# Local attention in a software pipeline: outputs moved one step later and behind the scores

## What is computed

```python
for i in range(DEPTH):                                            # 6 layers, 16 heads of 64
    x = attn_layer(shift_tokens(x), Wqkv[i], q_scale[i], k_scale[i], Wo[i]) + x
    x = ffn_layer(shift_tokens(x), ln_g[i], ln_b[i], W1[i], b1[i], W2[i], b2[i]) + x
# attn_layer: q, k, v = x @ Wqkv; q, k normalised by head, scaled, rotated
# each window of 32 queries sees its own 32 keys and the 32 before (masked to a band of 33)
sim = jnp.einsum('bhwie,bhwje->bhwij', bq, bk2) * QK_SCALE
attn = jax.nn.softmax(jnp.where(mask, -big, sim), -1)
out = jnp.einsum('bhwij,bhwje->bhwie', attn, bv2)                 # then out @ Wo
```

## Time and profile before

| what | value |
|---|---|
| median of three executions | 2394.74 us |
| the profiled execution | 2394.71 us |
| its span, first to last instruction | 2392.9 us |
| PE, matmuls | 2003.8 us (84%) |
| DVE | 1759.8 us (74%) |
| ACT | 1492.5 us (62%) |
| POOL | 1241.6 us (52%) |
| copies of line 822, first to last | 168.5 to 1916.4 us, 384 of them |

### The profile page before, as it was taken

How to read it: one execution, slowest core, us unless ns; L and a number is a source line. 1 busy time by engine, 2 the same in 40 slices (tenths; PEclk the granted TensorE clock), 3 DMA queues, 4 the chain that set the end, 5 groups by cost and what they waited for, 6 DMA issues and landing times. The chain is left out here.

```text
span 2392.9 us, 81109 instructions
## 1 busy us (share of the span) xinstructions
PE 2003.8 (84%) x33532; PEld 1489.2 (62%) x33532; DVE 1759.8 (74%) x3964; ACT 1492.5 (62%) x5173; POOL 1241.6 (52%) x869
## 2 busy tenths in 40 slices
PE   5549998999999999999998999989999964773377
PEld 2338767677676877758767577775877732432255
DVE  4568878688786887868778688786887837685754
ACT  2228768587685877858778587785877823451122
POOL 1138757477574776738767377673765701221000
PEclk8679999999999999999999999999999986885699
DMA  2011111021110211102111021110210100001000
GB/s 96 0 36 39 33 37 50 27 67 35 37 54 24 71 30 42 50 24 70 30 42 50 24 66 33 44 47 24 66 30 26 39 3 12 1 0 54 1 0 18
DMA packets 88157, 85.58 MB, mean 36 GB/s; under 512 B 15360, under 2 KB 82944, under 8 KB 87168
## 3 DMA queue, kind: packets, MB, share of 16 engines
q1 hardware_dynamic: 87808, 80.62, 11.9%
HBM read 25.51 MB, written 1.05 MB: 11 GB/s over the span
## 5 line engine op out<-in xcount | busy, mean ns | idle before, releaser
L1000 POOL TENSOR_TENSOR RN<-N,minus_half 128x8 f32<-128x8 f32 x384 | 632.7, 1648 | 179.8 <-DVE N L928 179.8
L840 ACT ACTIVATE PB<-PS,NMX 128x64 f32<-128x64 f32 x1536 | 462.0, 313 | 26.8 <-DVE NMX L948 10.0
L596 PE MATMUL PS<-WQ,XS 128*128 128x256 f32 x1536 | 434.5, 406 | 14.5 <-SPq L541 13.0
L995 POOL TENSOR_TENSOR RR<-R 128x512 f32<-128x512 f32 x192 | 244.6, 1274 | 151.6 <-DVE QK L958 151.6
L995 POOL TENSOR_TENSOR RR<-R1B,R2B 128x512 f32<-128x512 f32 x192 | 244.5, 1274 | 140.4 <-DVE QK L958 140.4
L840 ACT ACTIVATION_READ_ACCUMULATOR PB<-PS,NMX 128x1 f32 x1536 | 312.0, 203 | 0.0
L596 PEld LDWEIGHTS PS<-WQ,XS 128*128 128x128 f32 x1536 | 261.3, 190 | 69.8 <-SPq L541 13.3
L735 PE MATMUL PS<-XB,VS 64*64 64x32 f32 x6144 | 213.6, 223 | 91.4 <-ACT XB L817 91.4
L948 DVE TENSOR_REDUCE NMX<-PS 128x4 f32<-128x256 f32 x384 | 163.1, 425 | 172.2 <-PE PS L749 172.2
L735 PEld LDWEIGHTS PS<-XB,VS 64*64 64x64 f32 x6144 | 181.0, 134 | 147.1 <-issue 142.7
L958 DVE SCALAR_TENSOR_TENSOR QK<-RN,RR 128x512 f32<-128x512 f32 x384 | 261.9, 682 | 0.6 <-POOL RR L995 0.6
(11 more groups left out here) (212 smaller groups left out, 3715.0 us busy)
## 6 DMA issues: line engine op xcount, KB each, us to landing
VS<-XB SPq DMA_DIRECT2D x384, 96.0 KB, 2.1
VS<-XB SPq DMA_DIRECT2D x288, 32.0 KB, 2.6
WQ<-in_wqkv SPq DMA_DIRECT2D x40, 192.0 KB, 2.4
WO<-in_wo SPq DMA_DIRECT2D x6, 512.0 KB, 4.5
XS<-XT SPq DMA_DIRECT2D x10, 256.0 KB, 3.2
XS<-XT SPq DMA_DIRECT2D x10, 255.8 KB, 4.8
BIG<-in_wgu SPq DMA_DIRECT2D x1, 2048.0 KB, 8.3
W<-in_w SPq DMA_DIRECT2D x6, 341.0 KB, 4.2
```

The costliest lines, as they stand in the source:

```text
L596: mm = nc.tensor.matmul(PQ[:, m % 2, j * 256:(j + 1) * 256], XSb[b][:, t0:t0 + P], WQ[:, pair * 384:pair * 384 + 256], start=True, stop=True)
L840: ex = nc.scalar.activation(PB[:, g % 2, u, :], SC[:, h, DH * t:DH * t + DH], ACT.Exp, bias=NMX[:, u:u + 1], accum_out=PSUMS[:, g % 2, u:u ...
L995: nc.gpsimd.tensor_tensor(RR[:, :, :], R1k[(g + 1) % 2][:, :, :], R2k[(g + 1) % 2][:, :, :], ALU.add)\
L1000: nc.gpsimd.tensor_tensor(RN[:, g % 2, :], N2[:, g % 2, :], minus_half[:, :], ALU.pow)
```

## The change

In a step, the matmuls of the outputs now belong to chunk g-3 (before: g-2) and come behind the scores (before: ahead of them); the values that are projected in step g are those of chunk g (before: g+1). The transposes of q and k always come first, then those of the probabilities and the values. ACT copies in the order TQ (822), PO (828, now chunk g-4), PX (817); before it was PX, TQ, PO. SP waits on `vp_in`, the copy itself, in place of `v_in`, which is gone. PE's wait for the copy of PX moves to just ahead of the next use of PX, in the next step. The feed-forward part moves from g % 32 == 1 to 2, its second down projection to another bank, and the loops run one step longer. No operation is added to or taken from a chunk.

```diff
-                return (k // B, k % B) if k >= 0 and g % SLOT == 1 else None
+                return (k // B, k % B) if k >= 0 and g % SLOT == 2 else None
-            WOUT, TOKS, FEAT, DOWN = (2, 5), (3, 5), (4, 2), (5, 0)
+            WOUT, TOKS, FEAT, DOWN = (2, 5), (3, 5), (4, 2), (5, 1)
@@ SyncE
                         if there(g + 1):
-                            sp.wait_ge(v_in.sem, v_in.take())
+                            sp.wait_ge(vp_in.sem, g + 2)
@@ TensorE: project_qk, feed_forward
-                        if m > SLOT and m % SLOT == 6:
+                        if m > SLOT and m % SLOT == 7:
                         project(0, range(PAIRS))
+                        if probs:
+                            pe.wait_ge(vp_in.sem, vp_in.peek(1))
                         project(1, range(3))
@@ TensorE: step
-                        values, probs, ffn, tail = (there(g + 1), there(g - 2), feed_forward_at(g),
+                        values, probs, ffn, tail = (there(g), there(g - 2), feed_forward_at(g),
...
-                        if tail:
-                            qk_to_features()
-                            values_and_probabilities()
-                        else:
-                            values_and_probabilities()
-                            qk_to_features()
+                        if there(g):
+                            pe.wait_ge(qk_in.sem, qk_in.take())
...
+                            tr.then_inc(qkt_ps.sem, 1)
                         if tail:
+                            pe.wait_ge(gelu_free.sem, gelu_free.peek(2))
+                        if there(g - 1) or there(g - 3):
+                            pe.wait_ge(vp_in.sem, vp_in.take())
+                        if there(g - 3):
+                            pe.wait_ge(vs_in.sem, vs_in.take())
+                        if probs:
+                            pe.wait_ge(pn_in.sem, pn_in.take())
...
-                        if values or probs:
-                            pe.wait_ge(vp_in.sem, vp_in.take())
-                        if values:
-                            pe.sem_inc(v_in.sem, 1)
-                        if probs:
-                            c = (g - 2) % CH
-                            if g - 2 > 0:
-                                pe.wait_ge(o_free.sem, o_free.take())
...
-                            mm.then_inc(o_ps.sem, 1)
                         if there(g):
                             c = g % CH
                             pe.wait_ge(qkt_in.sem, qkt_in.take())
...
                             mm.then_inc(sc_in.sem, 1)
+                        if there(g - 3):
+                            c = (g - 3) % CH
+                            if g - 3 > 0:
+                                pe.wait_ge(o_free.sem, o_free.take())
...
+                            mm.then_inc(o_ps.sem, 1)
@@ ScalarE
+                    def outputs(m):
+                        l, b, pair, c = where(m)
+                        act.wait_ge(o_ps.sem, o_ps.take())
...
                     def step(g):
-                        values, probs = there(g + 1), there(g - 2)
-                        if values or probs:
...
-                            nc.scalar.activation(XB[:, (g + 1) % CH, cols], PX[:, cols], ACT.Copy)\
-                                .then_inc(vp_in.sem, 1)
+                        values, probs = there(g), there(g - 2)
                         if there(g):
...
                                 TQ.rearrange("p (k s) -> p k s", k=2), ACT.Copy).then_inc(qkt_in.sem, 1)
-                        if there(g - 2):
...
+                        if there(g - 4) and not feed_forward_at(g - 1):
+                            outputs(g - 4)
+                        if values or probs:
...
+                            nc.scalar.activation(XB[:, g % CH, cols], PX[:, cols], ACT.Copy)\
+                                .then_inc(vp_in.sem, 1)
...
                         if feed_forward_at(g):
+                            outputs(g - 3)
                             feed_forward(*feed_forward_at(g), g)
@@ all engines
-                    for g in range(-3, TOTAL + 3):
+                    for g in range(-3, TOTAL + 4):
```

More of the change, by code:

```diff
@@ L578, in _ @@
                                 load_layer(done[0] + 1)
-                    for f in (wq_dma, v_in, vs_dma, qks_free, layer_dma, qks_dma):
+                    for f in (wq_dma, vs_dma, qks_free, layer_dma, qks_dma):
                         f.settle(sp)
@@ L610, in feed_forward @@
                     def feed_forward(l, b, g):
+                        probs = there(g - 2)
                         def project(h, heads):
@@ L673, in step @@
                             project_qk(g + 3)
[L674 to L681, removed]
@@ new lines, in step @@
+                        if tail:
+                            pe.wait_ge(gelu_free.sem, gelu_free.peek(2))
[5 more added lines that the diff above has]
+                            pe.wait_ge(pn_in.sem, pn_in.take())
+                            for h in range(2):
+                                last = nc.tensor.transpose(
+                                    PX[:, 256 + h * P:256 + (h + 1) * P],
+                                    PB[:, g % 2, 2 * h:2 * h + 2, :].rearrange("p t k -> p (t k)"),
+                                    ident[:, :])
@@ new lines, in step @@
+                        if values:
+                            l, b, pair, c = where(g)
+                            for j in range(CB):
+                                t0 = (CB * c + j) * P
+                                last = nc.tensor.matmul(PX[:, j * P:(j + 1) * P], XSb[b][:, t0:t0 + P],
+                                                        WQ[:, pair * 384 + 256:(pair + 1) * 384],
+                                                        start=True, stop=True)
+                        if values or probs:
+                            last.then_inc(vp_ps.sem, 1)
@@ L754, in step @@
                             mm.then_inc(sc_in.sem, 1)
+                        if there(g - 3):
+                            c = (g - 3) % CH
+                            if g - 3 > 0:
+                                pe.wait_ge(o_free.sem, o_free.take())
+                            for w in range(4):
+                                for t in range(2):
+                                    for h in range(2):
+                                        keys = slice(2 * WIN * t, 2 * WIN * t + 2 * WIN)
+                                        vals = VX if w % 2 else VS
+                                        cols = 256 + P * h + WIN * w
+                                        mm = nc.tensor.matmul(
+                                            PO[DH * h:DH * h + DH, t, WIN * w:WIN * w + WIN],
+                                            vals[keys, c, w // 2, DH * h:DH * h + DH],
+                                            XB[keys, (g - 1) % CH, cols:cols + WIN],
+                                            start=True, stop=True)
+                            mm.then_inc(o_ps.sem, 1)
                         if ffn:
@@ L824, in step @@
                                 TQ.rearrange("p (k s) -> p k s", k=2), ACT.Copy).then_inc(qkt_in.sem, 1)
-                        if there(g - 2):
[L826 to L830, removed]
-                                PO[:, :, 0:P].rearrange("p t (j q) -> p t j q", j=CB), ACT.Copy)\
-                                .then_inc(o_free.sem, 1)
+                        if there(g - 4) and not feed_forward_at(g - 1):
+                            outputs(g - 4)
+                        if values or probs:
+                            cols = slice(0 if values else 256, 512 if probs else 256)
+                            act.wait_ge(vp_ps.sem, vp_ps.take())
+                            nc.scalar.activation(XB[:, g % CH, cols], PX[:, cols], ACT.Copy)\
+                                .then_inc(vp_in.sem, 1)
                         if there(g + 3) and not feed_forward_at(g - 1):
```

40 lines of the change are left out of this document (8 added, 32 removed).

## The result

The changed kernel takes 2314.18 us in the median of four executions (2312.12 to 2317.25) against 2393.4 us (2388.17 to 2403.46): a ratio of 0.9665, 95% interval 0.9631 to 0.9699. That is 79 us less, against 51 forecast. The profiled execution has a span of 2310.3 us, 82.6 less.

A forecast was written before the change was run, and what follows sets the result against it. It took a wait passed around PE, DVE and ACT (3.57 us a step), with SP's slower transfer loop beside it, as the bound. Gains of 17.7 + 28 + 5 = 51 us gave 2344 us; own range 2332 to 2364, wide 2300 to 2383.

The forecast's parts named there:

- rival 1: SP's transfers: long landings become short and SP keeps up; 2251 us, chance 0.08, or partly, 2297 us, another 0.12.
- The wait in mid-step: PE's wait for the copy of PX ahead of the outputs: removed, the step shrinks by 0.32 us to 3.25.
- `sem_inc` on PE: PE's signal to SP: dropping it saves SP a hop of at most 0.14 us, only when SP isn't late.
- Slots 0 and 11: Slots without weights to bring in: SP's 3.27 us holds, 0.30 us gained a step, 17.7 us in all.
- Slots 2, 4, 6, 8, 10: Slots starting with a burst of transfers: SP sets the pace after it, 3.35 us a step; 28 us gained.
- Slots 1, 3, 5, 7, 9: Slots already paced by SP at 3.90 us a chunk: 1 us gained each, 5 us in all.
- SP's 3.27 and 3.90 us a chunk: SP's serial loop of issue, landing wait and remainder: 3.27 us a chunk, 3.90 in odd slots with weight loads.
- part of the way: SP's landings shorten only partly, at most half the full effect: 2297 us, chance 0.12.
- The smaller margin of SP: Values needed 8.0 instead of 9.2 us later: SP may fall behind about 4.7 us instead of 5.9.
- Rivals 2, 3 and 4: Another engine takes the wait (2375 us, 0.17); SP's loop lengthens (2463 us, 0.06); SP paces even slots too (2377 us, 0.07).
- the signs named: Slot 0 and 11 steps 3.25 to 3.3 us, no idle before outputs, SP waits some 60 us, slot 9 about 105.

The follow-up runs named there:

- e10: Changed kernel with PE itself waiting for landings, plus DVE normalising only 8 of 64 columns of each block of probabilities: 2253.37 us, step 3.257 us.
- e11: Changed kernel with PE waiting for landings and less DVE normalising, plus ACT copying only the first half of TQ: 2252.44 us, step 3.257 us.
- e3: Kernel before, with PE counting up `v_in` behind the scores instead of ahead of the outputs: 2387.17 us, ratio 0.9986.
- e9: Kernel before, without PE's `sem_inc` on `v_in`; SP waits on `vp_in`, the copy of PX, instead: 2369.49 us, ratio 0.9909.
- e2: Kernel before, with four landing semaphores on which PE itself waits, so SP no longer waits for landings: 2368.1 us, ratio 0.9908.
- e1: Changed kernel, with four landing semaphores on which PE itself waits, so SP no longer waits for landings: 2254.26 us, ratio 0.9437.
- e4: Changed kernel, with SP also waiting for the end of the step's exponentials, so it issues later: 2351.12 us, ratio 0.9837.
- e8: Kernel before, with only the outputs (still of chunk g-2) moved behind the scores: 2598.3 us, ratio 1.0877.

## Why the prediction was right, and where it wasn't

The median of 2314 us lies below the forecast's own range, 2332 to 2364, and inside the wide one, 2300 to 2383, in a part that it held open for rival 1.

- **The wait in mid-step** goes, and the steps are 3.257 us against 3.25 forecast. The value is right, but half of its reason is wrong, so that the two agree is partly luck. I took the loop transposes, copy of TQ, scores, outputs, projection (3.25) for the bound, above PE's own 3.18 us. By e10 and e11, which take DVE and the copy of TQ out of it, what is left is PE's own pace, 3.257. So of the 0.386 us of idle time in the weight loads that I took off as wait, some 0.07 us (3.257 - 3.18) is nothing that an earlier copy could remove.
- **`sem_inc` on PE** was the mis-priced part: 0.10 us of each step (e3, e9), not nothing. It made's 0.14 us from copy to outputs out of 0.05. The sum isn't off by it, as the new step was added up anew; but the prediction put the whole gain of the step down to the order, and 33 of the 114 us between e2 and e1 are this instruction's.
- **Slots 0 and 11** were to gain 17.7 us and gained 20.0: SP didn't even hold them at 3.27.
- **Slots 2, 4, 6, 8, 10** were to gain 28 us and gained 32.8.
- **Slots 1, 3, 5, 7, 9** were to gain 5 us and gained 30.1. This is the term that was mis-sized: 25 of the 32 us by which the forecast falls short of the profiled execution's 82.6. Its step was that SP's 3.27 and 3.90 us a chunk stay (and 109 less the margin of 5.9 is 103, 3 us off the 106.4 that it was called near). They didn't: in these slots the wait for landing fell from 1.91 to 1.65 us a chunk, and issue and wait together from 3.20 to 2.98 us, and 5 slots x 28 chunks x 0.22 = 31 us is the gain. That was rival 1, in part, whose outcome "part of the way" had 0.12. Against its place, the moment of the issue, the prediction held that nothing shown ties the long landings to a moment; e3 and e9 show the tie in slot 0, and the sorted chunks have it in the other slots. That it explains the gain of these slots isn't shown: in e9 and e3 issue and wait also fell there, to 3.09 and 3.07 us, and the slots took 753.9 and 767.3 us, against 755.5 before. This stays open.
- **The smaller margin of SP** isn't shown by itself. Longer steps rose from 30.3 to 63.5 us, but they are counted over a usual step that is 0.31 us shorter; and e4, with 1.6 us less of margin again and 108.7 us, has longer landings too.
- **Rivals 2, 3 and 4** didn't come. ACT's and DVE's play sufficed (e10), and the mean wait for a landing fell, though the longest rose from 3.7 to 4.3 us.
- Of the signs named, the steps of 3.25 to 3.3 us in slot 0 and the outputs without idle time came, and the waits for SP rose to 46 us (60 named). The 0.10 us ahead of the scores aren't a wait for the copy of TQ (e11), and slot 9 took 101.2 us, not 105.

## What to carry to other kernels

When three engines are each some 90% busy in a step and none is full, look for the loop that the wait travels in, and let the consumer use a copy that is one step old. Then look what else stands between: an order of the work is one piece, and single parts of it can cost more than the whole gains (205 us in e8, against 79). A queue that waits for each transfer before it issues the next is a bound of its own; a semaphore for each buffer and the wait at the consumer took 60 us off the changed kernel here, and 24 us off the kernel before.

## What was not expected of the hardware

- A `sem_inc` of PE between a wait and the matmuls behind it lengthens the path by 0.10 us (3.567 to 3.471 and 3.476 us a step, e3 and e9).
- Pairs of transfers within on-chip memory land on average 1.36 to 1.97 us after SP begins to wait in slot 0, by the moment in the step at which they are issued, and 1.39 to 2.37 us in slots 1 to 10.
- PE's weight loads have a gap of 0.10 us at the change from 128*128 to 64*32, with nothing to wait for (e11, 205.43 to 205.53 us).
